# Layer 1 of a fused two-layer attention kernel: last unit's biased sums at the batch's end, heads projected ahead of turned queries, floors and key scaling on GpSimd, fourth unit's scores by rows

## The reference, cut to what matters

```python
# layer 1 attention (per batch), then a dense FFN with ternary weights
xn = ln(x, g_norm)
q = l2norm((xn @ Wq).heads) * q_scale            # 16 heads x 64
k = l2norm(concat([null_k, k]))  * k_scale       # one k for all heads
sim = einsum('bhid,bjd->bhij', q, k) * 8 + rel_pos_bias
attn = softmax(where(causal & mask, sim, -max))
x = x + ffn(ln((attn @ concat([null_v, v])) @ Wout, g_out))
# layer 2 attention: no l2norm, another bias; then a top-2 mixture of 8 experts
x = x + moe(layernorm(attention2(x), g_out))
```

## Time and profile before

| | before |
|---|---|
| runs, median (lowest to highest) | 578.08 us (577.95 to 581.03) |
| the profiled execution's own time, its span | 581.05 us, 579.3 us |
| granted TensorE clock over the span | 0.938 |
| busy share of the span: PE, DVE, ACT, POOL | 84%, 73%, 65%, 52% |
| busy in 48.07 to 152.95 (nine batches of layer 1) | of 104.88 us: PE 101.75, DVE 96.91, ACT 90.59, POOL 65.45 |

### The profile page before, as it was taken

The page is one execution under the profiler, slowest core; times in us unless marked ns, Lnnn a source line. Parts: engine busy times, 40 slices in busy tenths (PEclk is TensorE's granted clock), DMA queues, the critical chain, the costliest instruction groups (busy, mean ns, idle before and its releaser), DMA issues.

```text
span 579.3 us, 13792 instructions
## 1 busy us (share of the span) xinstructions
PE 485.3 (84%) x3220; PEld 391.4 (68%) x3220; DVE 422.1 (73%) x2148; ACT 375.2 (65%) x1475; POOL 303.6 (52%) x368
## 2 busy tenths in 40 slices
PE   2778999999999889979899999989778139999930
PEld 1456777777777676758688888868666127878730
DVE  3889999999999896877978888887796503343413
ACT  1568889888888876747798888967763004344410
POOL 4486666665646724775353343425766512555650
PEclk9779999999999999989999999999978759999975
DMA  5451016721100000000111210000111121323117
GB/s 166 97 182 24 20 26 130 152 78 44 43 5 5 9 4 2 0 1 9 45 42 44 79 42 8 5 6 21 33 39 40 36 64 36 85 56 83 35 39 217
DMA packets 54696, 29.73 MB, mean 51 GB/s; under 512 B 19884, under 2 KB 51572, under 8 KB 54644
## 3 DMA queue, kind: packets, MB, share of 16 engines
q1 hardware_dynamic: 48900, 22.09, 15.6%
q0 software_dynamic: 2560, 4.90, 2.7%
q10 hardware_dynamic: 3184, 2.16, 1.2%
HBM read 16.13 MB, written 10.90 MB: 47 GB/s over the span
## 4 chain that ended last, share of the span: by engine, by line
PE 58%; issue 11%; DVE 9%; POOL 7%; ACT 7%; DMA 5%; SPq 1%; ACTq 0%; DVEq 0%; POOLq 0%
PE psS L888 10%; PE psA L943 8%; PE psS L1193 6%; PE psT L906 5%; PE psO L924 4%; PE psQ L843 4%; PE psQ L859 4%; PE psQ L1183 3%; ACT sc L1296 2%; PE psO L914 2%; DVE sc L1590 2%; PE psO L915 2%; DMA slot_rows<-Y,dest_u 2%; ACT qT L1279 2%; PE psA L1183 1%
## 5 line engine op out<-in xcount | busy, mean ns | idle before, releaser
L1296 ACT ACTIVATE sc<-sc,negmax 128x97 f32<-128x97 f32 (+3 forms) x512 | 179.0, 354 | 26.0 <-DVE negmax L1590 25.5
L637 POOL TENSOR_TENSOR wide_buf<-bias,mask 128x132 f32<-128x132 f32 (+3 forms) x128 | 100.2, 799 | 97.5 <-DVE pn L1605 84.0
L888 PE MATMUL psS<-kk,qT 128*128 128x194 f32 (+3 forms) x512 | 102.1, 321 | 7.9 <-DVE negmax L1590 7.8
L1590 DVE CUSTOM_DVE_ANT_0 sc<-psS,wide_buf 128x97 f32<-128x97 f32 (+3 forms) x512 | 93.6, 238 | 17.5 <-PE psS L888 13.1
L888 PEld LDWEIGHTS psS<-kk,qT 128*128 128x128 f32 x512 | 79.6, 194 | 28.6 <-issue 25.1
L1296 ACT ACTIVATION_READ_ACCUMULATOR sc<-sc,negmax 128x1 f32 x512 | 97.6, 191 | 0.0
L584 POOL TENSOR_TENSOR qrn<-qssc,half 128x9 f32<-128x9 f32 (+1 forms) x32 | 55.5, 1735 | 41.8 <-DVE qssc L1576 41.7
L1605 DVE TENSOR_TENSOR pn<-sc,rsum 128x128 f32<-128x128 f32 (+3 forms) x128 | 64.9, 507 | 6.0 <-DVE rsum L1599 0.2
L943 PE MATMUL psA<-Wo,OT 128*128 128x128 f32 (+1 forms) x512 | 66.4, 285 | 0.8 <-DVE OT L1617 0.8
L943 PEld LDWEIGHTS psA<-Wo,OT 128*128 128x128 f32 x512 | 63.8, 199 | 1.8 <-DVE OT L1617 1.2
L1617 DVE TENSOR_SCALAR OT<-psO,cols 128x512 f32<-128x512 f32 x64 | 47.6, 744 | 2.6 <-PE psO L924 1.8
(11 more groups left out here) (298 smaller groups left out, 1009.7 us busy)
## 6 DMA issues: line engine op xcount, KB each, us to landing
slot_rows<-empty SPq DMA_DIRECT2D x2, 1390.0 KB, 10.5
xb<-slot_rows SPq DMA_DIRECT2D x16, 139.0 KB
vp_u<-vp SPq DMA_DIRECT2D x128, 8.0 KB, 1.7
choice_rows<-zero_row SPq DMA_DIRECT2D x8, 256.0 KB, 3.1
wide_buf<-choice_rows SPq DMA_DIRECT2D x8, 256.0 KB, 5.2
vp_u<-vp SPq DMA_DIRECT2D x64, 16.0 KB, 1.8
eW<-in_L_ffn_W SPq DMA_DIRECT2D x4, 256.0 KB, 3.0
gT<-in_L_ffn_W SPq DMA_DIRECT2D x4, 256.0 KB, 3.3
```

Source lines behind the costliest of these rows:

```text
L637: pool.tensor_tensor(unit_masked(i, u).rearrange("p h e k -> p (h e) k"), unit_bias(layer, u).rearrange("p h e k -> p (h e) k"), mask[laye ...
L888: m = pe.matmul(score_bank(u, h), qT[i][:, h, u].rearrange("p m q -> p (m q)"), kk[i][:, :, 0:w], start=True, stop=True)
L1296: m = act.activation(v, v, ACT.Exp, bias=negmax[:, u, g:g + 1], scale=-1.0, accum_out=psum_row[:, u, g:g + 1])
L1590: dve.tensor_tensor_reduce(sc[u][:, h, e, :], score_bank(u, h)[:, e * WIDTH[u]:(e + 1) * WIDTH[u]], unit_masked(i, u)[:, h, e, :], -1.0, - ...
```

## The change

- PE: in a round of layer 1, the first half of the heads of b+1 is projected first, ahead of the turned queries of b; the first half of the turned queries of b+1 is issued between the third unit's scores and the values of b-1, not at the round's end.
- Fourth unit, both layers: four matmuls of 64 rows and 129 columns instead of two of 128 rows and 258. The two halves of the rows write different banks, and all four wait for the third unit's biased sums.
- DVE: the fourth unit's biased sums stand at the end of their own batch's round, behind `divide` of unit 2, instead of in the next one. The floors and the scaling of the keys are gone from DVE.
- GpSimd: takes the floor ahead of each power, and scales the keys by their norm behind the first power of the batch.
- ACT: the constant scale of the keys (`k_col`, a column) is applied in the copy to `kk`; the two halves of the query copy are apart, the first between the exponents of units 2 and 3, the second behind the squares of the heads' first half; the key's square comes behind that.
- Setup: two DMAs on SyncE and two operations of DVE on `kqs`, and two of the three for the null key, go; one for `k_col` comes.

```diff
+        def score_part(u, h, e):
+            w = WIDTH[u]
             if u == UNITS - 1:
-                return psS[:, 1 - h, 0:2 * w]
-            return psS[:, u % 2, 2 * w * h:2 * w * (h + 1)]
+                return psS[:, 1 - e, w * h:w * (h + 1)]
+            return score_bank(u, h)[:, e * w:(e + 1) * w]
+        def in_order(u):
+            return [(0, 0), (1, 0), (0, 1), (1, 1)] if u == UNITS - 1 else [(0, 0), (0, 1), (1, 0), (1, 1)]
 ...
             def q_rsqrt(b, h):                                  # POOL
-                apart(pool, (s["q_floor"], 2 * b + h + 1))
+                apart(pool, (s["ss_step"], 2 * b + h + 1))
+                pool.tensor_scalar(qssc[:, lo:hi], qss[:, lo:hi], 1e-24, None, ALU.max).then_inc(s["q_floor"], 1)
+                pool.wait_ge(s["q_floor"], 2 * b + h + 1)
                 rsqrt(qrn[:, lo:hi], qssc[:, lo:hi], hi - lo, s["rn_ready"])
+            def keys_in(b, i):                                  # POOL
+                pool.wait_ge(s["v_read"], b + 1)
+                pool.wait_ge(s["rn_ready"], 2 * b + 1)
+                held(pool, s["kT_psum"], b - 1)
+                pool.tensor_tensor(kd[i][:], kvs[:, 0:DH].unsqueeze(1).broadcast_to([P, 2, DH]),
+                                   qrn[:, 0:1].unsqueeze(2).broadcast_to([P, 2, DH]), ALU.mult).then_inc(
+                    s["k_ready"], 1)
 ...
             def project_heads(b, h, i):                         # PE
+                if h == 0:
+                    pe.wait_ge(s["xnT_ready"], b + 1)
                 held(pe, s["q_ready"], 2 * b + h - 1)
 ...
-                      (s["scores_ready"], 4 * (n - u) if u < 2 else 4 * (n - 1)))
+                      (s["scores_ready"], 4 * (n - u) if u < 2 else 4 * (n - 1) if u == 2 else 4 * n))
+                if u == UNITS - 1:
+                    for h in range(2):
+                        for e in range(2):
+                            rows_of = slice(DH * e, DH * (e + 1))
+                            m = pe.matmul(score_part(u, h, e), qT[i][rows_of, h, u].rearrange("p m q -> p (m q)"),
+                                          kk[i][rows_of, e, 0:w], start=True, stop=True)
 ...
                 def batch(b, i):                                # PE
+                    if not last:
+                        project_heads(b + 1, 0, 1 - i)
                     turn_queries(b, 1)
                     if not last:
                         project_values(b + 1, 1 - i)
-                        project_heads(b + 1, 0, 1 - i)
 ...
+                    if not last:
+                        turn_queries(b + 1, 0)
                     if not first:
                         values(b - 1, 1 - i)
                     scores(0, b, 3, i)
 ...
                         turn_keys(b + 1, 1 - i)
-                        turn_queries(b + 1, 0)
                     turn_pair(b, i)
 ...
-                act.copy(kk[i][0:DH, 0, 1:P + 1], psA[0:DH, k0:k0 + P])
-                act.copy(kk[i][DH:P, 1, 1:P + 1], psA[DH:P, k0:k0 + P]).then_inc(s["kk_ready"], 1)
+                for e in range(2):
+                    half_of = slice(DH * e, DH * (e + 1))
+                    m = act.activation(kk[i][half_of, e, 1:P + 1], psA[half_of, k0:k0 + P], ACT.Copy,
+                                       scale=k_col[half_of, 0:1] if layer == 0 else 1.0)
 ...
                 def batch(b, i):                                # ACT
-                    queries(0, b, i)
+                    if not last:
+                        squares(b + 1, 0)
+                    queries(0, b, i, (1,))
+                    if not last:
+                        square_keys(b + 1)
                     if not first:
                         pair_T(b - 1, 1 - i)
-                    if not last:
-                        squares(b + 1, 0)
 ...
                     weights(4 * b + 1, 1)
+                    if not last:
+                        queries(0, b + 1, 1 - i, (0,))
                     weights(4 * b + 2, 2)
 ...
                     if reads:                                   # DVE
                         outputs(b - 2, 1, i, True)
-                    if not first:
-                        biased(n - 1, 3, 1 - i)
 ...
                         values_in(0, b + 1, 1 - i)
-                        floored(b + 1, 0)
                     biased(n, 0, i)
 ...
-                    if not last:
-                        floored(b + 1, 1)
                     biased(n + 2, 2, i)
 ...
-                    if not last:
-                        keys_in(b + 1, 1 - i)
 ...
                     divide(b, 1)
+                    biased(n + 3, 3, i)
```

More of the change, by code:

```diff
@@ L1260, in squares, with square_keys, queries @@
                 held(act, s["ss_step"], 2 * b)
-                if h == 0:
-                    act.wait_ge(s["kv_psum"], b + 1)
-                    act.activation(qsq[:, 0, :], psA[:, P:P + DH], ACT.Square)
                 act.wait_ge(s["q_psum"], 2 * b + h + 1)
-                act.activation(qsq[:, 1 + 8 * h:9 + 8 * h, :], psQ[:, h, :].rearrange("p (h d) -> p h d", d=DH),
-                               ACT.Square).then_inc(s["sq_ready"], 1)
-            def queries(layer, b, i):
+                m = act.activation(qsq[:, 1 + 8 * h:9 + 8 * h, :], psQ[:, h, :].rearrange("p (h d) -> p h d", d=DH),
+                                   ACT.Square)
+                if h:
+                    m.then_inc(s["sq_ready"], 1)
+            def square_keys(b):
+                act.wait_ge(s["kv_psum"], b + 1)
+                act.activation(qsq[:, 0, :], psA[:, P:P + DH], ACT.Square).then_inc(s["sq_ready"], 1)
+            def queries(layer, b, i, halves=(0, 1)):
                 B = b + NB * layer
                 held(act, s["scores_psum"], 4 * B - 4)
-                for h in range(2):
+                for h in halves:
                     if layer == 0:
@@ L1288, in keys_T @@
                 k0 = KT_AT[layer]
[L1289 to L1290 removed]
+                if no(B, 0):
+                    act.wait_ge(s["k_col_ready"], 1)
+                for e in range(2):
+                    half_of = slice(DH * e, DH * (e + 1))
+                    m = act.activation(kk[i][half_of, e, 1:P + 1], psA[half_of, k0:k0 + P], ACT.Copy,
+                                       scale=k_col[half_of, 0:1] if layer == 0 else 1.0)
+                m.then_inc(s["kk_ready"], 1)
             def weights(n, u):
[L1293 to L1295 removed]
+                for k, (h, e) in enumerate(in_order(u)):
+                    g = 2 * h + e
+                    act.wait_ge(s["scores_ready"], 4 * n + k + 1)
+                    v = sc[u][:, h, e, :]
                     m = act.activation(v, v, ACT.Exp, bias=negmax[:, u, g:g + 1], scale=-1.0,
@@ L1344, in attention_first @@
                 ternary_abs()
+                input_T(0, 1, 1)
+                queries(0, 0, 0, (0,))
                 keys_T(0, 0, 0)
-                input_T(0, 1, 1)
                 over(act, NB, batch, 2, 2)
@@ L1587, in biased @@
                 apart(dve, (s["probs_ready"], n - 3), (s["bias_ready"], n + 1), (s["scores_psum"], n + 1))
-                for g in range(4):
-                    h, e = g // 2, g % 2
-                    dve.tensor_tensor_reduce(sc[u][:, h, e, :], score_bank(u, h)[:, e * WIDTH[u]:(e + 1) * WIDTH[u]],
+                for h, e in in_order(u):
+                    g = 2 * h + e
+                    dve.tensor_tensor_reduce(sc[u][:, h, e, :], score_part(u, h, e),
                                              unit_masked(i, u)[:, h, e, :],
@@ L1722, in batch @@
                         moments(b - 2, i)
-                    if not last:
-                        keys_in(b + 1, 1 - i)
-                    else:
+                    if last:
                         dense_stats(1)
```

46 lines of the change are left out of this document (15 added, 31 removed).

## The result

The changed kernel takes 583.59 us (median of 6, 582.76 to 585.60) against 578.10 (577.91 to 581.03): a ratio of 1.0082, interval 1.0060 to 1.0104. Forecast were 576.3 and a range of 569 to 582. Its profiled execution took 584.10 with a span of 582.3.

The account below looks back on a forecast made before the run. A loop through several engines was taken to bound layer 1. Layer 1 -1.0, layer 2 -1.8 and edges +1.0 made -1.8 us, from 578.08 to 576.3, forecast chance .48; the range was 569 to 582.

Parts of the forecast that it names:

- -.08 per batch: Layer 1's loop: changes of -.42, -1.04, +.92 and +.46 us summed, counted in 13 of 16 batches, about -1.0.
- heads to reciprocal: Layer 1's link from heads to the fourth unit's reciprocal: 3.49 to 4.41 us, +.92, as ACT copies precede the exponents.
- The .19 ... which I let fall away.: Reciprocal's .19 us lag behind the fourth unit's exponents, put down to DVE's first unit and left out of the new link.
- Fourth scores by rows: Link from fourth scores to input turn on PE: four overlapping pairs, .46 plus .15 us, .61 instead of 1.03, -.42.
- R2: Rival: half-row matmuls don't run beside each other, fourth scores take 1.07 us; 584.6 us in all, chance .14.
- Heads first: Link from input turn to heads on PE: heads need xnT alone, 1.02 instead of 2.06 us, -1.04.
- Edges: Layer 1's end .85 us later with sums before the projection, start about +.15 for GpSimd's power; together +1.0.
- Layer 2: Fourth scores by rows end about .36 us earlier; at best -.13 x 14 = -1.8 us, at worst none.
- R1: Rival: DVE's queue bounds layer 1, so .66 us less work per batch is won; 568.7 us, chance .22.
- R3: Rival: sums at the batch's end delay queries_norm and the turned queries, about .3 us per batch; 581.2 us, chance .16.
- The .15 of margin: Layer 1: turned queries can go 1.76 us behind the fourth scores' end, while heads hold PE until 1.9.
- costs nothing as long as the values stand ahead of them: Fourth unit's four matmuls all waiting for the third unit's sums add no time with the values ahead on PE.

Follow-up runs that it names:

- a_norows: The changed kernel with the fourth unit's scores as two matmuls of 128 rows again; 586.77 us, ratio 1.0139 to the kernel before.
- a_noorder: The changed kernel with the order of heads, turned queries, squares and query copies on PE and ACT as before; 587.71 us, ratio 1.0163.
- b_rowsL2: The kernel before with the fourth unit's scores by rows in layer 2 only; 578.93 us, ratio 0.9989.
- a_noP: The changed kernel with the floors and the scaling of the keys on DVE again; 582.24 us, ratio 1.0064 to the kernel before.
- a_noS: The changed kernel with the fourth unit's sums in the next batch again, behind norm, divide and outputs; 583.13 us, ratio 1.0074.
- b_rows: The kernel before with the fourth unit's scores by rows in both layers and nothing else; 579.79 us, ratio 1.0002.
- pair_fill: The changed kernel with the pair's copy ahead of the squares and eight weight turns of Wo moved into PE's wait behind layer 1; 577.15 us, ratio 0.9962.
- a_pairfirst: The changed kernel with one move: ACT copies the turned pair ahead of the squares; 579.20 us, ratio 1.0009 to the kernel before.
- a_fill: The changed kernel with eight weight turns of the second layer's Wo moved into PE's wait behind layer 1's last fourth scores; 579.88 us, ratio 1.0013.
- b_fill: The kernel before with the eight weight turns of Wo moved into PE's wait behind layer 1; 577.44 us, ratio 0.9989.
- b_fill2: The same kernel as b_fill, run and profiled a second time; 578.20 us, ratio 0.9987.

## Why the prediction was wrong

The mechanism was right, a loop through PE, ACT and DVE sets layer 1's period, and the sign was not: the sum of -.08 per batch was smaller than the errors of its terms. Its terms were mis-sized, and nearly all to the same side: the turn before was taken .10 too long, and in the new turn heads to reciprocal .05, fourth scores to input turn .06 and input turn to heads .05 too short. And the sum of the edges had no term for the fall of the clock.

- *The turn before.* I walked the batch from 151.56, 11.61 us. The eleven batches have 11.39 to 11.63, 11.51 in the mean; mine was near the long end (first link 1.03, where .97 is usual; reciprocal .28 behind the end of the last exponents, where .17 is usual). Everything new was priced against a turn .1 too long.
- *"The .19 ... which I let fall away."* Heads to reciprocal came to 4.46, forecast 4.41. Of the .19 between the read-out of the exponents' sum and the reciprocal, .03 is left (146.74 + .19 to 146.96). But in the kernel before it was .07 in seven of the eleven batches, so less fell away than the prediction took. The other pieces are right to .02: square to exponents was worked out at 1.61 and measured 1.62.
- *Fourth scores by rows.* .67 for .61: eight matmuls of 64 rows in .72, so two do run beside each other, and rival R2 falls. Four pairs at .115 leave .2 for all the rest of the link, where I took .15 for the change of mode. Of the rule from the Trainium skill, TensorEngine Tiling (Array Packing), Key Properties, this agrees with the half on tiles that work in parallel; the .2 is in line with a drain at the change of mode, but no row separates a drain from the rest of the link.
- *Heads first.* 1.03 and 1.12 in alternate batches, 1.07 in the mean, forecast 1.02: from the end of ACT's `xnT` to the heads it is .05 in the one and .14 in the other (142.00 + .37 to 142.51), where I took .05 for all.
- Together -.08 became +.17 per batch: 13 x .17 = 2.2, of 2.35 measured.
- *Edges.* The .85 behind the sums came, about .8 (a_norows). At the start the third batch's fourth scores are .5 earlier, where .15 later was forecast. That the clock would fall there, for another 1.5 or so, was in no term. It is the larger part of the 2.3 (a_noorder, with the same waits and no fall, is 1.4 to 1.6 shorter). What makes it fall stays open, as said above.
- *Layer 2.* -1.8 was forecast "at best". The middle seven turns are 72.2 before and 71.3 after, -.13 each, the forecast size, in both pairs of profiles; but the forecast had it all from the rows, and they alone give .09 (b_rowsL2), while .07 comes without them (71.72 in a_norows). Over the whole layer it can't be told from nothing.
- *R1* (DVE is the bound) falls with a_noP, and *R3*, the sums that push the norm out, with a_noS. The .15 of margin held in the loop (PE takes the turned queries at 143.47, .28 after the norm ends at 142.50 + .69 = 143.19). In the order of before it would not have held (a_noorder).
- *"costs nothing as long as the values stand ahead of them"* was right for the changed order alone, and wrong as a reason: in b_rows the values do stand ahead, and the wait costs .21. In the changed kernel it is the turned queries that hide it.

Open: loop, sums and clock at the edge come to 4.6, the other stages give back up to 1.3 in the profiles, and yet the medians lie 5.2 to 5.5 apart. The runs of the changed kernel have a lower mean clock (0.929 and 0.933 against 0.941), but so has pair_fill (0.933), which is faster; the mean alone explains nothing, and where else the clock fell in the unprofiled runs isn't seen. Nor is it shown why it falls behind layer 1 in one kernel or execution and not in another.

## What to carry to other kernels

Write the loop as links between starts, and take each link's mean over many turns before pricing an edit against it: here one batch's reading was off by more than the whole forecast gain. An edit that frees one link (heads ahead) hands its time to the next engine in the loop unless the work that moves behind it has a wait to fill; the pair's copy, put into ACT's wait, gave .28 per batch for one moved line. At the end of a loop, look for PE's idle time as well as for what it delays, since the work behind it may then run at the lower clock. Independent matmuls that are due later can fill it: that was worth 1.3 us of the stretch where the clock fell all the same (pair_fill against a_pairfirst) and 2.5 where it did not (a_fill against the changed kernel). And don't take one profile in which the clock stayed up for a proof that the wait was the cause: the next kernel with the same waits had the fall.

## What the runs showed of the hardware

- Two matmuls of 64 rows into two banks overlap: eight of 129 columns in .72 us, against 1.14 for four of 258 with 128 rows.
- Small work was dearer on GpSimd but did not lengthen the turn: key scaling 401 ns (264 for the same product on DVE in a_noP), a floor of 9 columns 250 ns (167 on DVE before).
- Behind waits of PE of 1.57 and 1.01 us with little between them the clock fell to the lower level in the changed kernel (both profiles), and in a_noorder it did not; with .55 and 1.01 it did not in a_fill and did in pair_fill. In one kernel (b_fill, b_fill2) a fall came in one execution and not in the other. A fall cost 1.4 to 1.6 us of a stretch.
